# Fp16 parts for half of the value products of the first attention layer: one core of a Trainium2, a blind prediction and its test

## The reference, cut to what matters

```python
q = (v @ WQ).reshape(B, S, H, C); k = (v @ WK)...; val = (v @ WV)...
scores = jnp.einsum('bshc,bthc->bsth', q, k) * SCALE
A = jax.nn.softmax(scores, axis=2)
u = jnp.einsum('bsth,bthc->bshc', A, val).reshape(B, S, H * C)
return u @ Wout + bout
```

## Time and profile before

| | |
|---|---|
| median of 3 runs | 4917.94 us |
| the profiled execution | 4918.01 us |
| its span | 4916.3 us |
| PE busy | 4586.0 us (93%) |
| DVE busy | 3655.1 us (74%) |
| ACT busy | 3150.1 us (64%) |
| POOL busy | 2325.2 us (47%) |
| mean granted TensorE clock | 0.967 |

### The profile page before, as it was taken

One profiled execution on the slowest core, in us unless ns is written; L12 is line 12 of the kernel. 1 busy time (PEld: TensorE's weight loads), 2 busy tenths in 40 slices (PEclk: granted clock), 3 DMA queues, 4 the chain that ended last, 5 costly groups with the idle time before them and its releaser, 6 DMA issues. The chain is left out here.

```text
span 4916.3 us, 106442 instructions
## 1 busy us (share of the span) xinstructions
PE 4586.0 (93%) x42579; PEld 2033.3 (41%) x42579; DVE 3655.1 (74%) x6356; ACT 3150.1 (64%) x3450; POOL 2325.2 (47%) x2279
## 2 busy tenths in 40 slices
PE   5999969999999999999999979999999999999965
PEld 3433423333333333333333334444444444444433
DVE  4677756666666666666666678888888888888878
ACT  2444426666666666666666638888888888888844
POOL 3455553333333323233333346666666666666656
PEclk9999979999999999999999979999999999999966
DMA  4212100000000000000000000000000000000001
GB/s 102 69 52 69 35 1 1 1 1 1 1 1 1 1 1 1 1 1 1 1 1 1 1 1 2 2 2 2 2 2 2 2 2 2 2 3 2 2 7 28
DMA packets 43624, 51.44 MB, mean 10 GB/s; under 512 B 33416, under 2 KB 33544, under 8 KB 43144
## 3 DMA queue, kind: packets, MB, share of 16 engines
q1 hardware_dynamic: 40440, 44.03, 3.4%
q10 hardware_dynamic: 2704, 0.72, 0.1%
HBM read 39.73 MB, written 4.19 MB: 9 GB/s over the span
## 5 line engine op out<-in xcount | busy, mean ns | idle before, releaser
L1716 DVE TENSOR_REDUCE a_mp<-psum 128x1 f32<-128x512 f32 x2072 | 1324.8, 685 | 667.8 <-PE psum L1593 654.1
L2442 DVE TENSOR_REDUCE f_mp<-psum 128x1 f32<-128x512 f32 (+2 forms) x2352 | 1472.7, 684 | 187.1 <-PE psum L2264 171.0
L1561 ACT ACTIVATE a_prob<-psum,escale 128x1024 f32<-128x1024 f32 x1024 | 1086.3, 1110 | 524.6 <-PE psum L1642 524.6
L2224 ACT ACTIVATE f_prob<-psum,escale_f 128x1024 f32<-128x1024 f32 x1152 | 1247.2, 1112 | 217.1 <-PE psum L2341 108.4
L1650 PE MATMUL psum<-a_prob,a_v 128*64 128x512 f32 x4104 | 994.2, 605 | 0.0
L2078 POOL TENSOR_SCALAR f_hi<-f_raw,part 128x512 f16<-128x512 f32 x324 | 506.2, 1562 | 393.8 <-ACT f_raw L2182 387.5
L2264 PE MATMUL psum<-f_kf,f_qf 64*128 64x512 f16 (+2 forms) x3658 | 652.6, 307 | 40.1 <-DVE f_mp L2442 31.2
L1481 POOL TENSOR_TENSOR a_u<-a_og,a_inv 128x512 f32<-128x512 f32 x129 | 134.4, 1042 | 1167.4 <-DVE a_inv L1731 1167.4
L2354 PE MATMUL psum<-f_prob,f_vh 128*32 128x512 f32 (+3 forms) x6144 | 614.7, 495 | 9.3 <-DVE f_oc L2464 7.3
L2333 PE MATMUL psum<-f_qf,f_kf 64*128 64x512 f16 (+3 forms) x3074 | 505.5, 327 | 18.9 <-ACT f_og L2187 18.2
L1650 PEld LDWEIGHTS psum<-a_prob,a_v 128*64 128x64 f32 x4104 | 249.0, 136 | 505.1 <-issue 501.5
(11 more groups left out here) (448 smaller groups left out, 6942.4 us busy)
## 6 DMA issues: line engine op xcount, KB each, us to landing
idx<-in_itok_BS_dram SPq DMA_DIRECT2D x36, 512.0 KB, 6.0
idx<-in_itok_BS_dram SPq DMA_DIRECT2D x54, 256.0 KB, 6.9
idx<-in_x_dram SPq DMA_DIRECT2D x18, 256.0 KB, 3.6
a_qh<-a_rowT SPq DMA_DIRECT2D x258, 1.0 KB
out_dram<-h SPq DMA_DIRECT2D x16, 256.0 KB, 2.6
f_qf<-f_rowT SPq DMA_DIRECT2D x130, 4.0 KB, 1.7
wd<-in_L_ffn_Wd_dram SPq DMA_DIRECT2D x2, 256.0 KB
bd<-in_L_ffn_bd_dram ACTq DMA_DIRECT2D x16, 2.0 KB
```

The lines of the kernel that those rows point to most:

```text
L1561: act.activation(prob[:, part], k.psum[:, pair:pair + 2].rearrange("p b n -> p (b n)"), ACT.Exp, scale=k.escale[:]).then_inc(s.read, 1)
L1716: dve.tensor_reduce(mp[:, tg % 2, t + 4 * r, c:c + 1], bank_of(j + r), X, ALU.max)\
L2224: act.activation(prob[:, u % NPF], k.psum[:, pair:pair + 2], ACT.Exp, scale=k.escale_f[:])\
L2442: dve.tensor_reduce(side[:, at[0]:at[-1] + 1:step], bank_of(j + r)[:, 0:len(at) * width].rearrange("p (a b) -> p a b", b=width), X, ALU.ma ...
```

## The change

- `A_PARTS` becomes (2, 3), (0, 1), (6, 7), (4, 5), and `A_VALUES_AT` becomes (4, 6, 9, 10): the parts run in slots 4 and 6 of their step and 1 and 2 of the step after, where they ran in slots 2, 4, 6 and 1 of the step after.
- Key tiles 0, 1, 4 and 5 are halved: ACT copies `prob` to fp16 (`ph`), DVE (kt 1, 5) and POOL (kt 0, 4) take `prob - ph` as fp16 (`pl`), and PE multiplies three fp16 products `vl*ph + vh*pl + vh*ph` in place of the fp32 product. `vh`, `vl` are made once per sequence by POOL (`twice`).
- The exponential gets a constant bias from a tile (`level`, 6 ln 2), which cancels in the softmax.
- Item `out` moves from behind exp 3 to behind exp 4, and `copy_out` from behind exp 1 to behind exp 3.
- POOL gets a new order; the residual add of a head comes one step later.
- The work before the first step gets five more memsets and their count in the start waits.

```diff
-A_PARTS = ((0, 1), (2, 3), (4, 5), (6, 7))
+A_PARTS = ((2, 3), (0, 1), (6, 7), (4, 5))
+A_PART_OF = {kt: p for p, part in enumerate(A_PARTS) for kt in part}
+A_HALVED = {0: 0, 1: 1, 4: 2, 5: 3}
+A_LEVEL = 6 * math.log(2.0)
-A_VALUES_AT = (2, 4, 6, 9)
+A_VALUES_AT = (4, 6, 9, 10)
-A_EXTRA = {0: (('x', 0),), 1: (('q', 2),), 3: (('out', -1),)}
-A_COPY_AT = 1
+A_EXTRA = {0: (('x', 0),), 1: (('q', 2),), 4: (('out', -1),)}
+A_COPY_AT = 3
...
+                def twice(b, par, n):
+                    here = v[:, par, :, 0]
+                    pool.tensor_copy(vh[:, par], here).then_inc(s.p, 1)
+                    passed(pool, k.seen, s.p, n + 5)
+                    pool.tensor_tensor(vl[:, par], here, vh[:, par], ALU.subtract).then_inc(s.p, 1)
+                def halve(G, kt):
+                    at = A_HALVED[kt]
+                    passed(pool, k.seen, s.p_high, n_half(G, kt))
+                    pool.tensor_tensor(pl[:, at], prob[:, kt], ph[:, at], ALU.subtract).then_inc(s.p_low, 1)
...
+                pool.memset(ph[:], 0.0).then_inc(s.clear, 1)
+                pool.memset(pl[:], 0.0).then_inc(s.clear, 1)
+                pool.memset(vh[:, 1], 0.0).then_inc(s.clear, 1)
+                pool.memset(vl[:, 1], 0.0).then_inc(s.clear, 1)
+                pool.memset(level[:], A_LEVEL).then_inc(s.clear, 1)
...
 (POOL, each step)
+                        split_q(G + 2, (x + 2) % 4, n_stream(i, x, "q", 0))
+                        halve(G, 0)
+                        if G > 1:
+                            add(i * 2 + (x - 2) // HEADS, x % 2, G)
+                        if x % HEADS == 4:
+                            prepare_batch(b, (x // HEADS + 1) % 2, b * 6)
+                        if x % HEADS == 5:
+                            split_x(b, (x // HEADS + 1) % 2, n_stream(i, x, "x", 0))
+                        halve(G, 4)
                         if x % HEADS == 3:
                             squares(i * 2 + x // HEADS)
+                        if x % HEADS == 6:
+                            twice(b, (x // HEADS + 1) % 2, b * 6)
...
 (ACT, each exp)
                             act.activation(prob[:, part], k.psum[:, pair:pair + 2].rearrange("p b n -> p (b n)"),
-                                           ACT.Exp, scale=k.escale[:]).then_inc(s.read, 1)
+                                           ACT.Exp, scale=k.escale[:], bias=level[:]).then_inc(s.read, 1)
+                            if part in (1, 2, 5, 6):
+                                act.wait_ge(s.read, n_stream(i, x, "exp", part - 1))
+                                act.activation(ph[:, A_HALVED[part - 1]], prob[:, part - 1], ACT.Copy)\
+                                   .then_inc(s.p_high if part in (1, 5) else s.p_high_act, 1)
...
 (PE, values of a halved part)
+                        pe.wait_ge(s.p_low, n_half(G, A_PARTS[p][0]))
+                        pe.wait_ge(s.p_low_dve, n_half(G, A_PARTS[p][1]))
+                        for kt in A_PARTS[p]:
+                            at = A_HALVED[kt]
+                            for a, b in ((vl, ph), (vh, pl), (vh, ph)):
+                                for half in range(2):
+                                    last = pe.matmul(ps[A_SUM][halves(half)], lhsT=a[:, bp, kt],
+                                                     rhs=b[:, at, half * HALF:(half + 1) * HALF], ...)
...
 (DVE)
+                def low(G, kt):
+                    at = A_HALVED[kt]
+                    dve.wait_ge(s.p_high_act, n_half(G, kt))
+                    dve.tensor_tensor(pl[:, at], prob[:, kt], ph[:, at], ALU.subtract).then_inc(s.p_low_dve, 1)
...
+                            if u == 0 and i + x:
+                                low(i * AROUND + x - 1, 5)
+                            if u == 4:
+                                low(i * AROUND + x, 1)
```

More of the change, by code:

```diff
@@ L1 @@
 from contextlib import ExitStack
+import math
 import numpy as np
@@ L704, in layer0 @@
         E = {name: k.sem("l0_" + name) for name in L_EVENTS}
+        k.spent, k.spent_at = [E[name] for name in ("gT", "eg", "wT", "gturn")], PAIRS_
         def first(pair):
@@ L1345, in attention1 @@
         prob = sb("a1_prob", [P, NPB, S], F32)
+        ph = sb("a1_ph", [P, 4, S], FP16)
+        pl = sb("a1_pl", [P, 4, S], FP16)
+        vh = sb("a1_vh", [P, 2, T, C], FP16)
+        vl = sb("a1_vl", [P, 2, T, C], FP16)
+        level = sb("a1_level", [P, 1], F32)
         un = sb("a1_un", [P, HALF], F32)
@@ L1366, in attention1 @@
         s.q_split = k.sem("a1_q_split")
+        s.p_high, s.p_high_act, s.p_low, s.p_low_dve = k.spent
         s.inverse = k.sem("a1_inverse")
@@ L1394, in n_pv, with n_half @@
             return NAV * (G + 1) + p + 1
+        def n_half(G, kt):
+            return k.spent_at + 2 * (G + 1) + kt // 4 + 1
         def bank_of(j):
@@ L1499, in _ @@
                 pool.memset(v[:, 1], 0.0).then_inc(s.clear, 1)
-                pool.sem_inc(s.summed, 1)
-                pool.sem_inc(s.scaled, 2)
-                pool.wait_ge(s.clear, 6)
+                pool.memset(ph[:], 0.0).then_inc(s.clear, 1)
[3 more added lines that the diff above has]
+                pool.memset(level[:], A_LEVEL).then_inc(s.clear, 1)
+                pool.sem_inc(s.summed, 2)
+                pool.sem_inc(s.scaled, 3)
+                pool.sem_inc(s.p_low, 2)
+                pool.wait_ge(s.clear, 11)
                 prepare_batch(0, 0, 0)
+                twice(0, 0, 0)
                 split_x(0, 0, 1)
@@ L1509, in _ @@
                         G = i * AROUND + x
+                        b = i * 2 + x // HEADS + 1
+                        split_q(G + 2, (x + 2) % 4, n_stream(i, x, "q", 0))
[7 more added lines that the diff above has]
+                        halve(G, 4)
                         if x % HEADS == 3:
                             squares(i * 2 + x // HEADS)
[L1512 to L1521, removed]
+                        if x % HEADS == 6:
+                            twice(b, (x // HEADS + 1) % 2, b * 6)
+                add(NB - 1, 0, NB * HEADS)
                 add(NB - 1, 1, NB * HEADS + 1)
@@ L1545, in copy_out @@
                     act.activation(un[:], ps[A_SUM], ACT.Copy).then_inc(s.copied, 1)
+                act.sem_inc(s.p_high_act, 2)
+                act.sem_inc(s.p_high, 2)
                 for n, (kind, of, part) in enumerate(A_START_STREAM):
@@ L1549, in _ @@
                     read_out(0, -1, kind, of + 1, 2 * (n % 2))
-                act.wait_ge(s.clear, 6)
+                act.wait_ge(s.clear, 11)
                 for i in range(NB // 2):
@@ L1559, in _ @@
                                 continue
-                            act.wait_ge(s.pv, n_pv(G - 1, part // 2))
+                            act.wait_ge(s.pv, n_pv(G - 1, A_PART_OF[part]))
                             act.activation(prob[:, part], k.psum[:, pair:pair + 2].rearrange("p b n -> p (b n)"),
-                                           ACT.Exp, scale=k.escale[:]).then_inc(s.read, 1)
+                                           ACT.Exp, scale=k.escale[:], bias=level[:]).then_inc(s.read, 1)
[3 more added lines that the diff above has]
+                                   .then_inc(s.p_high if part in (1, 5) else s.p_high_act, 1)
                             if part == A_COPY_AT:
@@ L1643, in score, with values @@
                     return last
-                def values(x, p):
+                def values(G, x, p):
                     bp = (x // HEADS) % 2
+                    first, final = A_PARTS[0][0], A_PARTS[-1][-1]
+                    if A_PARTS[p][0] in A_HALVED:
+                        pe.wait_ge(s.p_low, n_half(G, A_PARTS[p][0]))
[5 more added lines that the diff above has]
+                                    last = pe.matmul(ps[A_SUM][halves(half)], lhsT=a[:, bp, kt],
+                                                     rhs=b[:, at, half * HALF:(half + 1) * HALF],
+                                                     start=(kt == first and a is vl), stop=(kt == final and a is vh and b is ph),
+                                                     skip_group_check=True)
+                        last.then_inc(s.pv, 1)
+                        return
                     for kt in A_PARTS[p]:
@@ L1651, in values @@
                                              rhs=prob[:, kt, half * HALF:(half + 1) * HALF],
-                                             start=(kt == 0), stop=(kt == T - 1), skip_group_check=True)
+                                             start=(kt == first), stop=(kt == final), skip_group_check=True)
                     last.then_inc(s.pv, 1)
@@ L1659, in _ @@
                 last.then_inc(s.pv, NAV - sum(at >= T for at in A_VALUES_AT))
-                pe.wait_ge(s.clear, 6)
+                pe.wait_ge(s.clear, 11)
                 for n, (kind, of, part) in enumerate(A_START_STREAM):
@@ L1684, in _ @@
                                             pe.wait_ge(s.read, n_stream(i, x, "exp", A_PARTS[p][-1]))
```

(8 more changed lines are left out.)

## The result

The changed kernel takes 5082.61 us (median of 4 runs, 5076.11 to 5084.04) against 4918.44 (4 runs) on the same chip: ratio 1.0332, 95% interval 1.0315 to 1.0350. It is slower by 164 us; forecast were 5085 and slower.

A forecast was written before the change was run, and what follows sets the result against it. PE, 99.9% busy, bound the kernel before; after the change a loop through PE and ACT would. 4918 + 166 (loop) - 8 (sums hidden) + 9 (memsets, last halved part) = 5085 us, range 5000 to 5160.

The forecast's parts named there:

- PE's saving: PE's halved parts: 1.42 us each against 1.86, 0.88 less per step, PE's own work falling to 15.46.
- ACT's prices: ACT's instructions: exponential with bias 1.20 us (1.09 in a row), fp16 copy 1.06 (0.95 in a row).
- Rival 2: ACT's copies to fp16 at half the price, three of them in the loop: 4901 us; chance 0.04.
- The loop: Alternation of PE and ACT over two bank pairs: 17.64 us per step, 1.30 more than 16.34, +166 us.
- the sums' extra would be hidden: One step in eight, with DVE's sums: its extra 0.47 us disappears in PE's new waits, -8 us in all.
- POOL's new order costs nothing: POOL's stream: two differences of 2.13 us per step, both ready before they are needed, so no added time.
- Its extra stays: Input step: PE's S x stands on the loop as it stood on PE before, so its extra time remains.
- DVE and POOL: Differences for the halved parts: 1.95 us each on DVE, 2.13 on POOL, in time; tile 5 by 0.5.
- Rival 1: PE stays the bound: ACT could run ahead, step 15.46 us, 4814 us in all; chance 0.09.
- The priced condition: For PE to stay the bound, 1.30 us must be missing from the 17.64 us loop; cheaper prices still gave 17.07.
- Rival 3: PE's clock falls to 0.88 because PE waits three times a step: +138, about 5223 us; chance 0.06.
- PE near 88% busy: Expected sign in the attention stage: PE's busy share near 88% at clock 1.00; over 97% would refute the prediction.

The follow-up runs named there:

- run 7: The changed kernel with all differences on DVE and POOL left out; 5069.93 us, ratio 1.0310 to the kernel before.
- run 10: Run 8 with copies of tiles 0 and 1 exchanged, slot 6's old order, POOL's preparation ahead of tile 0's difference, half of two big memsets; 4926.61 us, ratio 1.0017.
- run 1: The changed kernel without the exponential's bias tile; 5030.63 us, ratio 1.0232 to the kernel before.
- run 2: The kernel before with the exponential's bias tile and one small memset added; 4916.39 us, ratio 0.9999.
- run 5: Run 4 without the exponential's bias; 4933.93 us, ratio 1.0032 to the kernel before.
- run 6: The changed kernel without ACT's four fp16 copies per step; 4928.94 us, ratio 1.0027 to the kernel before.
- run 3: The changed kernel with ACT's fp16 copy of key tile 1 moved behind item out; 5033.20 us, ratio 1.0241 to the kernel before.
- run 4: Run 3 with the maxima's M of slot 2 moved ahead of the halved part; 4968.60 us, ratio 1.0105 to the kernel before.
- run 12: Run 10 without the bias and with POOL's difference of tile 0 ahead of the next sequence's preparation; 4862.89 us, ratio 0.9890 to the kernel before.
- run 8: The changed kernel with all four ACT copies moved later and PE's M earlier in slots 2 and 6; 5061.73 us, ratio 1.0293 to the kernel before.

## Why the prediction was right, point by point

- **PE's saving.** A halved part was put at 1.42 us; PE's timeline of the changed kernel has it from 1501.83 to 1503.25, 1.42. The fp32 parts kept 1.77 and 1.88 beside the earlier trace rows.
- **ACT's prices.** Put at 1.20 and 1.06, from the earlier trace rows:

```profile
L1602 ACT ACTIVATE a_prob<-psum,a_level,escale 128x1024 f32<-128x1024 f32 x1024 | 1205.3, 1204 | 350.8 <-PE psum L1687 350.8
...
L1606 ACT ACTIVATE a_ph<-a_prob 128x1024 f16<-128x1024 f32 x512 | 538.3, 1051 | 0.0
```

  By the rule of the Trainium skill (ScalarE: Activation LUTs, section "What ACT_TABLE_LOAD costs") it would be 1.23 for the exponential, which is too much, and 1.04 for the copy, which is as near to the measured 1.051 as mine. Rival 2, copies at half the price, falls with the measured copy.
- **The loop.** Put at 17.64, measured 17.56, in the order of the terms, with the forecast in brackets: 4.15 (4.13), 0.20 (0.21), 3.73 (3.73), 0.15 (0.21), 3.78 (3.76), 0.21 (0.21), 5.29 (5.28), 0.05 (0.11). PE's three waits, start against readiness, are 0.83 before out, 0.34 before exp 7 and about 0.8 before exp 1 (0.87, 0.34, 0.63). The last is longer because the M ahead of the slot 6 part took 0.31 and not 0.51.
- **That the sums' extra would be hidden** (-8 us) was wrong. The sums' step takes 18.25, 0.69 over the ordinary one, where the kernel before has 0.47: DVE's sums make PE's M in slot 4 late, and that M stands on the loop. I had taken PE's idle time as one store; it lies in three places, and this wait fell outside them. DVE, POOL and PE in such a step:

```profile
1477.78 0.56 DVE L1804 TENSOR_SCALAR mean_f<-mean_f 128x8 f32<-128x8 f32 x1
```

```profile
1477.28 1.04 POOL L1510 TENSOR_TENSOR a_u<-a_og,a_inv 128x512 f32<-128x512 f32 x1
```

```profile
1478.99 0.39 PE L1638 MATMUL psum<-a_xh,a_qh 64*128 64x512 f16 x1 [0.34 <-DVE a_mp L1775]
```

  DVE's small `mean_f` operation takes 0.56 where it takes 0.17 in the kernel before and in run 7, and it ends together with POOL's product, at 1478.3. These 0.39 us match the 0.40 that run 7 gives back; with that "POOL's new order costs nothing" was wrong by 6 us. "Its extra stays", of the input step, was wrong too: it and the step behind it have 1.02 and 0.09 over the ordinary step, where the kernel before has 1.17 and 0.27.
- **The sum is in part luck.** The sums' steps came out 11 us above their term and the two falls of the clock add 3; the loop's 0.08 per step (10 us) and the input steps (5 us) went the other way. That 5085 and 5082.61 agree to 2 us is more than the terms deserve; the loop's 1.22 of the forecast 1.30 us per step is what was right.
- **DVE and POOL.** Both differences were in time. DVE's took 1.28 on average (1.22 alone, up to 1.89 beside POOL), not 1.95 each. Run 7 bears out that they don't carry the ordinary step.
- **Rival 1 (PE stays the bound)** did not happen in this kernel, but it is a matter of order: run 10 has all of the change's work, with the bias and half of the two big memsets, and takes 15.90 per ordinary step, 0.44 under the kernel before. The priced condition, 1.30 us missing from the loop, was met by moving copies, not by cheaper ones. In time run 10 gained nothing (4926.61), because of its one long step in eight.
- **The clock** kept its higher level nearly throughout, with waits up to 0.66 us in every step, so Rival 3 did not happen at its size. It did fall in two of the 128 steps, both of them sums' steps, which then took 19.9 in place of 18.25. The second of them:

```profile
2330.00:2333.50 3.50, 2.80 (x26) 1.45 (x25) 3.43 (x8) 2.56 (x4) 3.23 (x3) 1.00 0.00 0
2333.50:2336.50 3.00, 3.00 (x12) 0.50 (x10) 2.21 (x3) 0.00 (x0) 0.00 (x0) 0.50 0.00 0
```

  Before it PE had waited 0.36 us for the copy of the sums and 0.34 for DVE's maximum. The other fourteen sums' steps have the same waits and no fall. The swing of which the Trainium skill tells (TensorE: Matmul & The Clock Gate, section "A second HAM failure mode: psum-queue depth-cycling") showed in these two steps alone, 3 us in all.
- "PE near 88% busy" came out as 93%: busy time counts the modelled ends of the last matmuls into each wait. From start to start PE's work is 17.56 - 0.83 - 0.34 - 0.81 = 15.58 us, 89% of a step.

Shown by experiment: that the bias costs by its place (runs 1, 2, 5), that the copies are nearly all of the loss where they stand (run 6), and that their place makes it (runs 3, 4 and 10, all with the same instructions on ACT and PE; run 12 without the bias). Read from the traces and not tested by a run of its own: that POOL's product holds DVE's `mean_f`. Open: why the clock falls in some of the steps with the same waits, and what run 12's order takes with the bias.

## What to carry to other kernels

When an engine is 99.9% busy and a change takes work from it, look for the next closed loop: follow one double buffer through both engines and add the spans in which each waits for the other. Here ACT's sum (forecast at 14.0 us) and PE's (15.5) lay both under the loop's 17.6. What is added to the engine beside costs by its place in the stream: in run 3 a copy moved behind the read that PE waits for took PE's wait for it away. And on an engine that goes in order, a wait moved later holds everything written behind it, as runs 8 and 10 showed on DVE and POOL.

## What the hardware showed beside

A DVE difference of two SBUF tensors and a POOL operation beside it take turns, as far as the times show: the one that starts later waits for the other. In the changed kernel:

```profile
1515.54 1.04 POOL L1470 TENSOR_TENSOR a_v<-h,mean 128x512 f32<-128x512 f32 x1
1516.76 1.80 POOL L1472 TENSOR_TENSOR a_v<-a_v,rstd 128x512 f32<-128x512 f32 x1 [0.18 <-POOL a_v L1470]
```

```profile
1515.77 1.89 DVE L1796 TENSOR_TENSOR a_pl<-a_prob,a_ph 128x1024 f16<-128x1024 f32 x1
```

POOL's first operation was under way when DVE's started, and kept its 1.04. DVE's ends at 1517.66, 1.08 behind the end of that one (1516.58), where it takes 1.22 alone. POOL's second starts meanwhile and ends 0.90 behind DVE's, where it takes 1.04 alone. In run 8 it is the same: POOL's difference, first, keeps 2.13 and ends at 1506.69; DVE's ends 1.08 behind it.

The second operation, POOL's product of 128 x 512 in the preparation, took 1.04 us in all 17 cases of the kernel before; in the changed one its minimum, median and maximum are

```profile
L1472 POOL TENSOR_TENSOR a_v<-a_v,rstd x17: 1043/1802/1809, 689.0 to 2941.2; 128x512 f32<-128x512 f32 x17
```

and with the differences left out (run 7) they are

```profile
L1472 POOL TENSOR_TENSOR a_v<-a_v,rstd x17: 1042/1042/1043, 688.8 to 2928.6; 128x512 f32<-128x512 f32 x17
```

DVE's maxima, which read PSUM, kept their mean of 0.685 us.
